# Feed-forward on one core: the down product from float32r halves, with the low half of h taken on GpSimd

## The reference, cut to what matters

```python
def fp4_linear(x, w):                       # both sides rounded to FP4 values in blocks of 16
    return jnp.einsum('bsk,nk->bsn', fp4_quant_dequant(x), fp4_quant_dequant(w))

x = _layernorm(x + attention(x))            # 8 x 1024 tokens, width H = 256, 16 heads
gate = fp4_linear(x, w_gate)                # to I = 704
y = fp4_linear(x, w_up)                     # to I = 704
h = jax.nn.silu(gate) * y
x = _layernorm(x + fp4_linear(h, w_down))   # back to 256: the "down" product
```

## Time and profile before

| | before |
|---|---|
| time, median of 3 runs | 1980.98 us (1980.68 to 1982.36) |
| span of the profiled execution | 1981.5 us |
| PE, DVE, ACT, POOL busy, share of the span | 97%, 93%, 83%, 38% |
| granted PE clock from 1600 to 1700 us | 1.00 |

### The profile page before, as it was taken

One profiled execution on the slowest core, in us unless ns is written; L12 is line 12 of the kernel. 1 busy time (PEld: TensorE's weight loads), 2 busy tenths in 40 slices (PEclk: granted clock), 3 DMA queues, 4 the chain that ended last, 5 costly groups with the idle time before them and its releaser, 6 DMA issues.

```text
span 1981.5 us, 43034 instructions
## 1 busy us (share of the span) xinstructions
PE 1931.0 (97%) x15806; PEld 1131.4 (57%) x15806; DVE 1845.4 (93%) x3236; ACT 1652.1 (83%) x3241; POOL 750.0 (38%) x747
## 2 busy tenths in 40 slices
PE   8999999999999999999999999999999999999998
PEld 7766444444444444444444444444478888888876
DVE  4788999999999999999999999999289999999997
ACT  6655889899898989989898988988967777777776
POOL 3000364666575353010001001000046666666785
PEclk9999999999999999999999999999999999999999
DMA  7985553355435435433543544353011111111210
GB/s 224 284 236 209 120 76 52 62 95 96 94 81 102 95 80 99 93 94 82 101 96 78 97 94 94 82 100 98 28 49 49 49 49 49 49 49 56 63 33 27
DMA packets 127199, 181.46 MB, mean 92 GB/s; under 512 B 37836, under 2 KB 82636, under 8 KB 126988
## 3 DMA queue, kind: packets, MB, share of 16 engines
q1 hardware_dynamic: 119308, 171.10, 37.6%
q10 hardware_dynamic: 7392, 7.34, 1.1%
q0 software_dynamic: 288, 0.27, 0.1%
HBM read 103.68 MB, written 73.40 MB: 89 GB/s over the span
## 4 chain that ended last, share of the span: by engine, by line
DVE 63%; PE 32%; issue 3%; DMA 1%; ACT 1%; SPq 0%; DVEq 0%; POOLq 0%; POOL 0%; ACTq 0%
DVE halfmax L1135 50%; PE ps L1401 10%; DVE halfmax L1130 7%; PE ps L1440 6%; PE ps L494 4%; PE ps L504 3%; PE ps L1389 2%; PE ps L1412 2%; PE ps L1045 1%; PE ps L1011 1%; PE ps L481 1%; PE ps L1448 1%; DVE room L1591 1%; PE ps L1457 1%; DVE room L1678 1%
## 5 line engine op out<-in xcount | busy, mean ns | idle before, releaser
L1096 ACT ACTIVATE room<-ps 128x512 f32<-128x512 f32 x2048 | 1084.4, 600 | 125.0 <-PE ps L1011 103.0
L1135 DVE TENSOR_REDUCE halfmax<-ps 128x1 f32<-128x512 f32 x1714 | 1039.5, 676 | 1.3 <-PE ps L986 1.3
L1011 PE MATMUL ps<-qs,ks 50*128 50x512 f32 x2048 | 716.4, 448 | 2.4 <-DVE halfmax L1135 1.3
L986 PE MATMUL ps<-ks,qs 48*128 48x512 f32 x1960 | 667.6, 437 | 23.8 <-DVE halfmax L1130 22.3
L1045 PE MATMUL ps<-room,vals 128*17 128x256 f32 (+2 forms) x8192 | 578.9, 384 | 0.3 <-ACT craw L1104 0.3
L986 PEld LDWEIGHTS ps<-ks,qs 48*128 48x128 f32 x1960 | 314.5, 185 | 423.6 <-DVE halfmax L1135 309.2
L164 POOL CAST mrow<-turned_rows 128x32 fp32r<-128x32 f32 x32 | 6.7, 210 | 904.2 <-DVE turned_rows L159 695.4
L1011 PEld LDWEIGHTS ps<-qs,ks 50*128 50x128 f32 x2048 | 327.2, 184 | 22.9 <-ACT room L1096 14.5
L1045 PEld LDWEIGHTS ps<-room,vals 128*17 128x17 f32 x8192 | 167.4, 96 | 232.9 <-issue 168.1
L1401 PE MATMUL ps<-wguT,xqT 128*128 128x512 f32 (+1 forms) x1152 | 268.4, 386 | 3.9 <-DVE xqT L1631 3.9
L1401 PEld LDWEIGHTS ps<-wguT,xqT 128*128 128x128 f32 x1152 | 212.0, 189 | 51.8 <-issue 9.9
(11 more groups left out here) (116 smaller groups left out, 2212.1 us busy)
## 6 DMA issues: line engine op xcount, KB each, us to landing
qk_parts<-parts SPq DMA_DIRECT2D x64, 512.0 KB, 3.9
qs<-qk_parts SPq DMA_DIRECT2D x192, 128.0 KB, 4.4
ks<-qk_parts SPq DMA_DIRECT2D x192, 128.0 KB, 7.1
ctx_raw<-craw SPq DMA_DIRECT2D x64, 256.0 KB
ready<-passing SPq DMA_DIRECT2D x27, 512.0 KB, 6.5
pairs<-ready SPq DMA_DIRECT2D x27, 512.0 KB
out_dram<-fin SPq DMA_DIRECT2D x64, 128.0 KB, 1.7
xin<-in_L_attn_x_dram ACTq DMA_DIRECT2D x14, 512.0 KB, 5.4
```

The costliest lines, as they stand in the source:

```text
L986: nc.tensor.matmul(ps[:, MX + max_number(i, u, bank) % 4, :], qs[rows, i.slot(RING), pair, t * P:(t + 1) * P], ks[rows, i.slot(RING), pair ...
L1011: nc.tensor.matmul(ps[:, score_bank(i, s, n), :], ks[rows, slot, pair, kt * P:(kt + 1) * P], qs[rows, slot, pair, qh * BANK:(qh + 1) * BAN ...
L1096: nc.scalar.activation(prob[:, prob_slot(i, s), score_order(i, s)[n], :], ps[:, score_bank(i, s, n), :], ACT.Exp, scale=float(D) ** -0.5). ...
L1135: nc.vector.tensor_reduce(halfmax[:, i.slot(2), bank, column:column + 1], ps[:, at + bank, :], AX.X, ALU.max, negate=True).then_inc(max_re ...
```

## The change

Down is done from float32r halves: h and w_down are each split into high and low, and high x high, high x low and low x high are summed, six chunks each, 18 products a tile in place of 5.5 float32 ones. The last 64 rows are a sixth full chunk (it repeats 64 rows of chunk five against weights of zero), so two tiles no longer share it. The high half of h comes from ACT, which now copies each piece of the transposed h twice: to `hT_half` (rounded) and to `hT` (whole). The low half is whole minus high, and a new POOL instruction makes it (`hT_split`). On PE the products with the high half (`down_high`) stand where down stood, the ones with the low half (`down_low`) behind gate and up. The low half of w_down is made once, on DVE, in the first three iterations.

```diff
@@ tensor @@
         def h_by_width(t):
             due(pe, "hq_ready", t.lin(1, 1))
+            wait(pe, sems["hT_whole"], t.lin(2))
...
-            for c in (4, 0, 1, 2, 3):
+            for c in (4, 5, 0, 1, 2, 3):
                 if c in (4, 0):
                     pe.wait_ge(sems["hT_ready"], t.lin(2, 1 if c == 4 else 2))
-                last = nc.tensor.matmul(ps[:, DN[t.slot(2)], 0:H], hT[:, c, :], wdT[:, c, :],
-                                        start=c == 4, stop=False)
...
+                for part in range(2):
+                    nc.tensor.matmul(ps[:, DN[t.slot(2)], 0:H], hT_half[:, 0, c, :], (wdT, wdT_low)[part][:, c, :],
+                                     start=c == 4 and part == 0, stop=False)
+
+        def down_low(t):
+            due(pe, "hT_split", t.lin(1, 1))
+            for c in range(IC):
+                last = nc.tensor.matmul(ps[:, DN[t.slot(2)], 0:H], hT_half[:, 1, c, :], wdT[:, c, :],
+                                        start=False, stop=c == IC - 1)
+            last.then_inc(sems["dn_psum"], 1)
...
-            wait(pe, sems["hT_ready"], min(t.lin(2, 1 - 2 * 3), 2 * NT))
+            wait(pe, sems["hT_whole"], min(t.lin(2, 1 - 2 * 3), 2 * NT))
...
-            for lag, stage in ((1, output_projection), (3, x1_by_width), (6, down), (3, gate_and_up), (5, h_by_width)):
+            for lag, stage in ((1, output_projection), (3, x1_by_width), (6, down_high), (3, gate_and_up), (6, down_low),
+                               (5, h_by_width)):
@@ scalar, copy_hT @@
-            nc.scalar.activation(hT[:, 4, :], ps[:, HT + 1, 0:P], ACT.Copy)
-            nc.scalar.activation(hT[rows, 5, :], ps[rows, HT + 1, P:2 * P],
+            due(act, "dn_psum", t.lin(1))
+            nc.scalar.activation(hT_half[:, 0, 4:IC, :].rearrange("p c n -> p (c n)"), ps[:, HT + 1, 0:2 * P],
                                  ACT.Copy).then_inc(sems["hT_ready"], 1)
+            due(act, "hT_split", t.lin(1))
+            nc.scalar.activation(hT[:, 4:IC, :].rearrange("p c n -> p (c n)"), ps[:, HT + 1, 0:2 * P],
+                                 ACT.Copy).then_inc(sems["hT_whole"], 1)
             act.wait_ge(sems["hT_psum"], t.lin(2, 2))
+            nc.scalar.activation(hT_half[:, 0, 0:4, :].rearrange("p c n -> p (c n)"), ps[:, HT, :],
+                                 ACT.Copy).then_inc(sems["hT_ready"], 1)
             nc.scalar.activation(hT[:, 0:4, :].rearrange("p c n -> p (c n)"), ps[:, HT, :],
-                                 ACT.Copy).then_inc(sems["hT_ready"], 1)
+                                 ACT.Copy).then_inc(sems["hT_whole"], 1)
@@ vector: split_wd(n), ahead of the first three iterations @@
+            dve.wait_ge(wt_ready, 2 * HC + n + 1)
...
+                nc.vector.tensor_tensor(wdT_low[:, 2 * n:2 * n + 2, :], across, wdT[:, 2 * n:2 * n + 2, :].bitcast(F32),
+                                        ALU.subtract).then_inc(sems["wd_split"], 1)
@@ gpsimd, behind the pairs operations and ahead of the power step of tile i-1 @@
+            t = i.plus(-6)
+            if t.ok(NT):
+                pool.wait_ge(sems["hT_whole"], t.lin(2, 2))
+                due(pool, "dn_psum", t.lin(1))
+                nc.gpsimd.tensor_tensor(hT_half[:, 1], hT[:, :, :], hT_half[:, 0].bitcast(F32),
+                                        ALU.subtract).then_inc(sems["hT_split"], 1)
```

More of the change, by code:

```diff
@@ L246, in build @@
         wguT = sb("wguT", [P, 2, HC, 2 * I], F32R)
-        wdT = sb("wdT", [P, (I + P - 1) // P, H])
+        wdT = sb("wdT", [P, (I + P - 1) // P, H], F32R)
         buffers = feed_buffers(sb)
@@ L1365, in sync, with chunk @@
             sp.wait_ge(stored[j], 16 * (NT // 2))
[L1367 to L1377, removed]
+    def chunk(a, c):
+        first = min(c * P, I - P)
+        return a[:, first:first + P]
     def tensor(pe, ks, cs=range(HC)):
@@ L1409, in h_by_width @@
             due(pe, "hq_ready", t.lin(1, 1))
+            wait(pe, sems["hT_whole"], t.lin(2))
             for c in (4, 5, 0, 1, 2, 3):
-                rows, columns = across(t, c)
-                last = nc.tensor.transpose(ps[rows, HT + c // 4, (c % 4) * P:(c % 4 + 1) * P],
-                                           hq[:, columns], ident[:, :])
+                last = nc.tensor.transpose(ps[:, HT + c // 4, (c % 4) * P:(c % 4 + 1) * P],
+                                           chunk(hq[:, :], c), ident[:, :])
                 if c in (3, IC - 1):
@@ L1417, in wd_across @@
         def wd_across(n):
-            pe.wait_ge(wt_ready, 2 * HC + n)
+            wait(pe, sems["wd_split"], n)
+            if n == 1:
+                pe.wait_ge(craw_ready, QH * NGR)
             for c in (2 * n, 2 * n + 1):
[L1422 to L1430, removed]
+                for o in range(HC):
+                    last = nc.tensor.transpose(
+                        ps[:, DN[0], (c % 2) * H + o * P:(c % 2) * H + (o + 1) * P],
+                        chunk(wd[:, o], c), ident[:, :])
@@ L1431, in wd_across, with down_high @@
             last.then_inc(wt_psum, 1)
-        def down(t):
+        def down_high(t):
             due(pe, "z_used", t.lin(1, -1))
             if t.k == 0:
-                pe.wait_ge(wt_ready, 2 * HC + IC // 2)
-            for c in (4, 0, 1, 2, 3):
+                pe.wait_ge(sems["wd_split"], IC // 2)
+            for c in (4, 5, 0, 1, 2, 3):
                 if c in (4, 0):
                     pe.wait_ge(sems["hT_ready"], t.lin(2, 1 if c == 4 else 2))
-                last = nc.tensor.matmul(ps[:, DN[t.slot(2)], 0:H], hT[:, c, :], wdT[:, c, :],
-                                        start=c == 4, stop=False)
[L1442 to L1449, removed]
+                for part in range(2):
+                    nc.tensor.matmul(ps[:, DN[t.slot(2)], 0:H], hT_half[:, 0, c, :], (wdT, wdT_low)[part][:, c, :],
+                                     start=c == 4 and part == 0, stop=False)
@@ L1537, in copy_wd @@
             act.wait_ge(wt_psum, 2 * HC + n + 1)
+            across = ps[:, DN[0], :].rearrange("p (c o) -> p c o", o=H)
             whole = min(2, IC - 1 - 2 * n)
-            last = nc.scalar.activation(wdT[:, 2 * n:2 * n + whole, :],
-                                        ps[:, DN[0], 0:whole * H].rearrange("p (c o) -> p c o", o=H), ACT.Copy)
-            for tile in range(0 if whole == 2 else 2):
-                rows = part_of(At(None, tile, U), IC - 1)
-                last = nc.scalar.activation(wdT[rows, IC - 1, :], ps[rows, DN[tile], H:2 * H], ACT.Copy)
+            last = nc.scalar.activation(wdT[:, 2 * n:2 * n + whole, :], across[:, 0:whole], ACT.Copy)
+            if whole < 2:
+                last = nc.scalar.activation(wdT[HALF:P, IC - 1, :], across[HALF:P, 1], ACT.Copy)
             last.then_inc(wt_ready, 1)
```

27 lines of the change are left out of this document (19 added, 8 removed).

## The result

The changed kernel takes 2086.6 us, median of 4 runs (2085.42 to 2088.61), against 1981.67 for the kernel before in 4 runs (1980.68 to 1982.49). The ratio is 1.0529, 95% interval 1.0517 to 1.0542: slower by 105 us. The forecast was 2079, its range 2052 to 2098. The profiled execution of after has a span of 2084.7 us and a time of 2086.47; in every run listed with both, the time is 1.8 us above the span.

A forecast was written before the change was run, and what follows sets the result against it. DVE bounds the feed-forward at 7.78 us of its own work, PE leading slightly every second iteration. 1981.0 us plus 71 (middle), 16 (last ten tiles), 5 (ramp) and 6 (drain), +98, gave 2079 us, range 2052 to 2098.

The forecast's parts named there:

- The main term: 48 middle tiles: POOL's split delays DVE's division of h by 1.64 us, 9.68 us a tile against 8.20, +71 us.
- in proportion: Division of h in the middle tiles: delay grows only with the POOL instruction's length, 1.37 us in place of 1.64.
- PE and ACT: Middle tiles: PE's tile goes to 7.77 us, idling almost 2; ACT's four copies take 1.68 us, their lateness hidden.
- The last ten tiles: Last ten tiles: the split holds up DVE's second sum for x by 1.6 us a tile, +16 us (14 to 20).
- The ramp: First three iterations: DVE waits for ACT's w_down copy, making x1's low half 1.7 us late each, +5 us (3 to 7).
- the clock in a rival alone: Middle tiles: 1.2 GHz in part of each iteration would use up PE's 2 us slack; within a 16% rival.
- The drain: End of the stage: four more delayed divisions of h, then the last tile's copies and split, +6 us (3 to 9).
- the base: Starting time before the change: profiled span 1981.5 us, median of the runs taken 0.5 lower, 1981.0 us.
- the rival: Middle tiles: the split precedes the division of x and both divisions follow it, some 0.2 us more an iteration, 2089 us; 16%.
- Division first: Middle tiles: DVE's division of h precedes the split, which then holds up the sum for x by 1.28 us; 2062 us, 13%.
- partly held: DVE in each iteration: the split delays it by only 0.3 to 1 us, 1985 to 2045 us; 4%.
- POOL yields: Middle tiles: DVE's steps go first and POOL's idle time takes the split; 1972 us or somewhat below, 4%.

The follow-up runs named there:

- the split alone: The kernel before plus one POOL subtraction of two 128x768 SBUF tiles where the change puts its split, result read by nobody: 2073.45 us.
- The half split: The changed kernel with POOL's split cut to 384 columns from 768, products using the low half's first three chunks twice: 2032.05 us.
- its three versions: The kernel before with an unread POOL subtraction (2073.45 us), with a POOL memset (1983.12 us), or with block scales reading one SBUF tile (1982.66 us).
- the version with the mended ramp: The changed kernel with w_down's low half taken on DVE behind x1's low half in the first three iterations: 2078.02 us.
- the version with the high half and the new scales: The changed kernel without h's low half (12 products, no POOL split), w_down's low half made behind x1's, scales reading one SBUF tile: 1973.47 us.
- the split behind xq: The changed kernel with POOL's split moved between xq and hg in its program: 2152.64 us.

## Why the prediction was right, step by step

**The main term.** +71 forecast, 70.4 measured, by the mechanism named: shown by the split alone, which has nothing else of the change. The split takes 2.06 us (1.83 plus a 0.21 wait forecast), the division of h 2.54 (2.3 to 2.6), 1.66 late (1.64); in 46 of the 48 tiles it takes 2.53 to 2.55. The half split settles how the delay grows: at a slope of 0.995 it is a full wait, not in proportion (which gave 1.37). The Trainium skill, SBUF — State Buffer, "Who interferes with whom", calls it an exclusive lock, and leaves a POOL instruction that only writes out of the contention; the rows agree with both, but for 0.13 us. By the rows the wait is 0.13 us shorter than the 2.06 - 0.27 = 1.79 of a full lock, since the division ends 0.75 behind the split's end and not 0.88.

**PE and ACT.** A product took the 0.12 us forecast from its columns, so down's 18 take 2.2 us. PE idles 1.58 us a tile (forecast almost 2). Its own time was forecast too low, without consequence: I took 2.26 us for the ten passes in every tile, but in the short iteration they take 1.97 (1608.95 to 1610.92). After the change PE's steps add up to an estimated 8.0 us, not 7.77: 7.09 from the transposes of x1 to the output projection (1642.26 to 1649.35) and 0.9 for the projection, its time before (1615.62 to 1616.52). Without the split the profile shows no idle time of PE at all from 1500 to 1850. So the saving in PE is small, and hidden by the split: without it 7.5 us are left, since DVE stands at 8.04, close behind PE's 8.20 before. ACT's four copies:

```profile
1641.48 0.36 ACT L1502 ACTIVATE hT_half<-ps 128x256 fp32r<-128x256 f32 x1
...
1642.96 0.40 ACT L1544 ACTIVATE xqT<-ps 128x256 fp32r<-128x256 f32 x1
```

They pass in 1642.96 - 1641.48 = 1.48 us where I took 1.68, and DVE does not wait for what follows.

**The last ten tiles.** +16 forecast, 17.7 measured. It is the second sum for x that stands behind the split, as argued (1.92 in place of 0.42 us). The forecast left out a second collision: with the split ahead of it, POOL's xq comes later and meets the sum for h on DVE, 1.30 in place of 1.03. Together 1.50 + 0.27 = 1.77 us a tile. DVE and POOL there:

```profile
2021.23 0.41 DVE L1593 TENSOR_TENSOR fq<-fq,xm 128x256 f32<-128x256 f32 x1
2021.32 1.99 POOL L1725 TENSOR_TENSOR hT_half<-hT,hT_half 128x768 fp32r<-128x768 f32 x1
...
2021.68 1.92 DVE L1668 TENSOR_TENSOR fq<-fq,xm 128x256 f32<-128x256 f32 x1
...
2024.24 0.62 POOL L1736 TENSOR_TENSOR fq<-fq,blocks 128x256 f32<-128x256 f32 x1
...
2024.31 1.30 DVE L1593 TENSOR_TENSOR room<-room,hm 128x704 f32<-128x704 f32 x1
```

**The ramp, the term that was mis-sized.** +5 (3 to 7) forecast, 8.0 measured. DVE's lateness was priced right. From the first gate and up to the second, before took 7.15 us and after 10.44, +3.3: 1.7 of lateness and 1.55 of a burst that takes 5.67 us instead of 4.13. Two bursts more than before run so, 3.1 us together if all of it comes through. The half split confirms the lateness: there the first burst runs at the full clock, and the second begins 8.89 us behind the first, 1.74 more than before. The clock's part differs from one execution to the next: with the same idle times ahead, the first burst is slow in three of the five traces with this ramp, and of the four traces with the ramp of before only the one of before has a slow third burst. Counted from the first output projection, this ramp costs 7.7 us against the trace of before and 8.7 to 9.6 against its three versions, so 8.0 is a low reading. I had the clock in a rival alone, and there for the middle, where it stays at 1.00 in spite of PE's idle time; it belonged into the ramp, for which the earlier trace rows showed a stretch at 0.68.

**The drain.** +6 forecast, 7.1 measured; the products wait for the split up to 3.5 us:

```profile
2068.46 0.97 PE L1441 MATMUL ps<-wdT,hT_half 128*128 128x256 f32 x6 [3.52 <-POOL hT_half L1725]
```

The terms are 5 us short of the 103.2 in span. The rest of the 7.6 us is the base. The prediction set a span, 1981.5, beside times. With the 1.8 us that lie between the two, the profiled execution of before took about 1983.3, which is 1.6 above the median of the four runs and not 0.5, and that median is 0.7 above the one of the three.

**The rivals.** The split came ahead of the division of x in the first two of the 48 tiles only. There it took 1.84 us, the 1.83 of the forecast without a wait. In the one the scales stood behind it (1.34 us), in the other the division of x (1.41), and the division of h took 0.88 in both. This cost DVE about 1 us a tile, less than the forecast case and not 0.2 more, as the rival had it. "Division first" and "partly held" are excluded by the other 46 tiles. "POOL yields" is excluded by every kernel with a split in this place.

**What stays open.** Why the scales with one SBUF input wait for hq: the same section of the Trainium skill counts `tensor_scalar` among the instructions that can, under conditions on their operands, enter a mode that takes the shared pair, which would do it; no run here separates that from another cause. And a POOL write as long as the split was not tried.

## What to carry to other kernels

Idle time on POOL is not free time: an instruction there that reads SBUF cost DVE its length here, less a head start, where it met a DVE instruction with two SBUF inputs, and it showed as a longer busy time and not as a wait. Before work is moved to POOL, look at what DVE does at that moment, and then at what is queued behind whoever waits for the result; moving the instruction out of the way cost more than the port did (2153 against 2087 us), until its result had a tile's time to arrive (2032). A saving on an engine that leads by little is worth only the distance to the next one.

## What the runs showed of the hardware that was not expected

- The clock in the ramp. After idle times of 2.46, 3.25 and 4.33 us just ahead of it, 18 products of gate and up took 5.6 to 5.7 us, at 0.66 to 0.71 granted on average; in the version with the mended ramp a burst after 2.64 us took 4.12 at 1.00. So the idle time directly ahead does not decide it alone, and the same idle time shows both: the burst after 2.46 us took 4.12 with half a split, and the one after 2.64 took 5.67 in the version with the high half and the new scales. 1.58 us of idle in every 9.7 us left the clock at 1.00; 2.2 us in every 10.7, with the split behind xq, left it at 0.95 on average.
- A `tensor_scalar` of 128x60 from one SBUF tile takes 0.45 us beside a POOL instruction that reads SBUF, as the form with two did (0.47); with none beside it, 0.18.
